# Two attention layers over 32 images: both lanes on one layer at either end, and the setup in parts

## The chip, the cores and the metric

The kernel runs on one core of a Trainium2 chip. The core has a matrix engine (TensorE, PE in the rows), VectorE (DVE), ScalarE (ACT), GpSimd (POOL) and SyncE (SP), which issues DMA transfers; each works through its own queue in order and they meet at semaphores. The metric is the device time of one execution in microseconds (us); lower is better.

## What is computed

x is 32 images of 128 channels by 32x32 pixels, float32. Two layers of self-attention follow one another:

```python
# layer 0
h = group_norm(x, 32 groups) * gn_w + gn_b
q, k, v = split(qkv_w @ h + qkv_b)                  # 128 channels each
attn = softmax(q^T k * C ** -0.5)                   # 1024 x 1024 for each image
x = x + proj_w @ (v attn^T) + proj_b
# layer 1
q, k, v = Wq @ x + bq, Wk @ x + bk, Wv @ x + bv     # 16, 16 and 128 channels
x = gamma * (v softmax(q^T k)^T) + x
```

## The kernel before

**Tiles.** One image has N = 1024 pixels; its attention is done in 8 tiles (TILES) of 128 rows of the 1024x1024 matrix. A tile runs through these steps: scores (TensorE, `score0` or `score1`) into a PSUM tensor `scores[l]` of 1024 columns; row maximum (VectorE, `row_max`, L498); exponent (ScalarE); a split into a float16 head and a float16 tail in `rows[l]`; a DMA transpose into a ring of four, `pt[l]` (SP, `swing`); 24 matmuls with V's head and tail (`attend`, L710 to L712); a division by the row sum (`invert` on VectorE, `norm` on ScalarE); a transpose back on TensorE (`back`, L731); and an addition on VectorE (`x1_out` or `y_out`). To keep float32's accuracy in float16 matmuls, each product of layer 0 is three matmuls (head by head, head by tail, tail by head).

**Lanes.** There are two lanes with buffers of their own. Lane 0 takes layer 0, lane 1 takes layer 1. Lane 0 puts its exponents into `prob` (L397), so that its scores are free right after, and splits on GpSimd (`head_row0` L300, `tail_row0` L305). Lane 1 writes its exponents over the scores (L402) and splits on ScalarE (L409) and VectorE (L512), so its scores are free only when the tail is done. `score0` (two halves of 512 columns, three matmuls each) and `score1` (two matmuls) are the layers' own.

**Slots.** The queue of each engine is written out slot by slot (an image has eight), in Python, with all loops unrolled. The constants of L33 to L42 say at which slot from the image's start a step stands: lane 0's tile t has its exponent in slot 8n+t, lane 1's in slot 8n+t+13 (EXP, L34); both lanes attend three slots after the exponent (L36) and add four after it (L37). Before image n's tiles come its load (-16), the statistics (-12, -11), two products for the group norm (-10, -9), the root (-8, GpSimd), `h` in float32 (GpSimd) and its head (ScalarE, -7), its tail (GpSimd, -6), four projections to q and k (-5, -4, -3, 0), each with a copy on ScalarE and a split on GpSimd, and V (1, 2). Layer 1's q and k are projected at 7 and 11, its V at 12 and 14. All layer-0 projections of q and k, the products of the norm and the transposes back go through one PSUM bank, `bank_t`; the V and layer-1 projections through another, `bank_w`.

**Order in a TensorE slot (L813 to L842).** Attend for both lanes; V or a layer-1 projection; q/k projection; norm product; the first half of lane 0's scores for the next slot, lane 1's scores, the second half of lane 0's; a wait until `bank_t` has been read; the transposes back. ScalarE's slot (L456) is lane 1's exponent and head, lane 0's exponent, the heads and copies out of PSUM, `h_head`, then the norms of both lanes.

**Setup.** Weights are loaded by SP behind image 0 (L258 to L267), turned by TensorE (`setup`, L796), scaled and split by VectorE (`setup`, L581); TensorE, VectorE and ScalarE do the whole of it between the first eight slots and all the others (L662, L844, L488 to L492).

## Time and profile before

| | us |
|---|---|
| median of 3 runs | 1636.66 |
| lowest and highest | 1635.16, 1637.1 |
| the profiled execution | 1633.07 |
| its span | 1630.8 |

The span is the time from the first to the last instruction of the profiled execution; 2.3 us lie around it. Busy time of the engines over the span: TensorE 1519.8, VectorE 1289.7, GpSimd 1247.4, ScalarE 1209.0 us. The page counts 43555 instructions and 305 MB of DMA, of which 512 transposes and 32 images in and out. The clock granted to TensorE was 0.988 of the full one on average. Time is best read by slots: the exponents (L397 for lane 0, L402 for lane 1) mark where each slot stands.

### The profile page before, as it was taken

How to read it: one execution, taken by the hardware profiler on the slowest of the kernel's cores; microseconds unless marked ns; L12 is line 12 of the kernel's file. 1: busy time of each engine (PE TensorE's matmuls, PEld its weight loads, DVE VectorE, ACT ScalarE, POOL GpSimd, SP SyncE). 2: the span in 40 equal slices, each digit the busy share in tenths (PEclk: the TensorE clock that was granted, in tenths of full speed). 3: DMA queues.
4: the chain of work that ended last, by engine and by line, in shares of the span. 5: the costliest groups of instructions: out<-in, count | busy, mean ns of one | idle time of the engine just before them, and what ended most of it. 6: DMA issues, size and time to landing. Idle time of an engine off the chain costs nothing.

```text
span 1630.8 us, 43555 instructions
## 1 busy us (share of the span) xinstructions
PE 1519.8 (93%) x16777; PEld 1102.4 (68%) x16777; DVE 1289.7 (79%) x2499; ACT 1209.0 (74%) x1697; POOL 1247.4 (76%) x1036
## 2 busy tenths in 40 slices
PE   3789999999999999999999999999999999999975
PEld 1557777767777677776767777677677777767754
DVE  2478888888888888888888888888888888887854
ACT  1467887777777777777777777877777877777753
POOL 3998888887888887787888788788878888877600
PEclk9999999999999999999999999999999999999987
DMA  1689999999999999999999999999999999999974
GB/s 47 117 143 200 196 198 201 209 192 201 195 201 204 198 196 196 197 198 192 203 203 204 203 190 204 198 198 205 190 203 194 195 205 197 203 189 186 195 137 97
DMA packets 1081437, 305.19 MB, mean 187 GB/s; under 512 B 1068273, under 2 KB 1068945, under 8 KB 1081233
## 3 DMA queue, kind: packets, MB, share of 16 engines
q1 hardware_dynamic: 1080080, 302.41, 106.1%
q8 instruction: 135, 2.21, 0.5%
q14 instruction: 70, 0.57, 0.1%
q10 hardware_dynamic: 1152, 0.00, 0.0%
HBM read 17.13 MB, written 16.78 MB: 21 GB/s over the span
## 4 chain that ended last, share of the span: by engine, by line
PE 48%; ACT 22%; DVE 16%; issue 10%; POOL 2%; DMA 1%; SPq 1%; ACTq 0%; POOLq 0%; DVEq 0%
DVE nmax L498 10%; ACT scores L402 9%; ACT prob L397 8%; PE mixed L710 7%; PE mixed L712 7%; PE mixed L711 7%; PE scores L671 6%; PE bank_w L778 4%; PE scores L673 4%; PE scores L672 4%; PE scores L696 3%; PE bank_t L731 2%; ACT v_head L452 2%; PE bank_w L768 2%; DVE qk L563 1%
## 5 line engine op out<-in xcount | busy, mean ns | idle before, releaser
L710 PE MATMUL mixed<-v_head,pt 128*128 128x129 f16 x4096 | 722.6, 223 | 4.5 <-DMA pt<-rows 4.3
L712 PE MATMUL mixed<-v_head,pt 128*128 128x129 f16 x4096 | 722.5, 220 | 0.0
L711 PE MATMUL mixed<-v_tail,pt 128*128 128x128 f16 x4096 | 722.2, 219 | 0.0
L498 DVE TENSOR_REDUCE nmax<-scores 128x1 f32<-128x1024 f32 x512 | 602.4, 1216 | 52.6 <-PE scores L696 32.3
L305 POOL TENSOR_TENSOR rows<-prob,rows 128x1024 f16<-128x1024 f32 x256 | 545.5, 2131 | 21.3
L402 ACT ACTIVATE scores<-scores,nmax 128x1024 f32<-128x1024 f32 x256 | 278.6, 1088 | 279.4 <-DVE nmax L498 279.4
L300 POOL TENSOR_SCALAR rows<-prob 128x1024 f16<-128x1024 f32 x256 | 267.9, 1046 | 227.3 <-ACT prob L397 210.8
L512 DVE SCALAR_TENSOR_TENSOR rows<-scores,rows 128x1024 f16<-128x1024 f32 x256 | 313.6, 1225 | 153.3 <-ACT rows L409 153.2
L711 PEld LDWEIGHTS mixed<-v_tail,pt 128*128 128x128 f16 x4096 | 407.0, 99 | 2.7
L710 PEld LDWEIGHTS mixed<-v_head,pt 128*128 128x128 f16 x4096 | 400.2, 98 | 7.0 <-DMA pt<-rows 6.6
L712 PEld LDWEIGHTS mixed<-v_head,pt 128*128 128x128 f16 x4096 | 398.1, 97 | 0.0
L397 ACT ACTIVATE prob<-scores,ebias 128x1024 f32<-128x1024 f32 x256 | 283.9, 1109 | 29.5 <-DVE ebias L503 25.9
L409 ACT ACTIVATE rows<-scores 128x1024 f16<-128x1024 f32 x256 | 262.2, 1024 | 23.7 <-ACT scores L402 0.4
L671 PE MATMUL scores<-qk_head 128*128 128x512 f16 x512 | 197.9, 387 | 48.7 <-ACT prob L397 47.9
L673 PE MATMUL scores<-qk_head,qk_tail 128*128 128x512 f16 x512 | 194.5, 380 | 0.0
L672 PE MATMUL scores<-qk_tail,qk_head 128*128 128x512 f16 x512 | 194.4, 380 | 0.0
L414 ACT ACTIVATE normal<-mixed,rinv 128x128 f32<-128x128 f32 x512 | 161.7, 371 | 22.3 <-DVE rinv L508 22.2
L671 PEld LDWEIGHTS scores<-qk_head 128*128 128x128 f16 x512 | 50.4, 99 | 158.5 <-issue 77.7
L364 POOL TENSOR_TENSOR qk_tail<-qk,qk_head 128x512 f16<-128x512 f32 x128 | 148.3, 1158 | 10.7
L731 PEld LDWEIGHTS bank_t<-ident,normal 128*128 128x128 f32 x512 | 69.7, 140 | 78.7 <-ACT normal L414 17.2
L696 PE MATMUL scores<-qk 64*128 64x512 f16 x512 | 100.5, 389 | 22.3 <-DVE rows L512 21.7
L731 PE MATMUL bank_t<-ident,normal 128*128 128x128 f32 x512 | 109.7, 286 | 6.7 <-ACT normal L414 6.6
(90 smaller groups left out, 1847.0 us busy)
## 6 DMA issues: line engine op xcount, KB each, us to landing
x_raw<-in_x_dram SPq DMA_DIRECT2D x32, 512.0 KB, 4.8
out_dram<-y SPq DMA_DIRECT2D x64, 256.0 KB, 3.0
pt<-rows SPq DMA_TRANSPOSE x512, 4.9
w_qkv<-in_L_conv_qkv_w_dram SPq DMA_DIRECT2D x3, 64.0 KB, 3.8
b_qk<-in_L_conv_bk_dram SPq DMA_DIRECT2D x8, 0.1 KB, 1.9
b_qk<-in_L_conv_bq_dram SPq DMA_DIRECT2D x8, 0.1 KB, 1.6
w_proj<-in_L_conv_proj_w_dram SPq DMA_DIRECT2D x1, 64.0 KB, 3.5
w_v<-in_L_conv_Wv_dram SPq DMA_DIRECT2D x1, 64.0 KB, 3.4
```

Of the source, the lines that this page charges most:

```text
L300: nc.gpsimd.tensor_scalar(rows[0][:, t % 2, 0, :], prob[:, t % 2, :], 1.0, 1.0, ALU.mult, ALU.mult).then_inc(row_headed[0], 1)
L305: nc.gpsimd.tensor_tensor(rows[0][:, t % 2, 1, :], prob[:, t % 2, :], rows[0][:, t % 2, 0, :], ALU.subtract).then_inc(row_tailed[0], 1)
L397: nc.scalar.activation(prob[:, t % 2, :], scores[0][:, :], ACT.Exp, bias=ebias[:, t:t + 1], scale=1.0).then_inc(exped[0], 1)
L402: nc.scalar.activation(scores[1][:, :], scores[1][:, :], ACT.Exp, bias=nmax[1][:, t:t + 1], scale=1.0).then_inc(exped[1], 1)
L409: nc.scalar.activation(rows[1][:, t % 2, 0, :], scores[1][:, :], ACT.Copy, scale=P_UP).then_inc(row_headed[1], 1)
L498: nc.vector.reduce_max(nmax[layer][:, t:t + 1], scores[layer][:, :], AX.X, negate=True).then_inc(maxed[layer], 1)
L512: nc.vector.scalar_tensor_tensor(out=rows[1][:, t % 2, 1, :], in0=scores[1][:, :], scalar=P_UP, in1=rows[1][:, t % 2, 0, :], op0=ALU.mult, ...
L671: mm(dst, a_head, b_head, start=start, stop=False)
L673: return mm(dst, a_tail, b_head, start=False, stop=stop)
L710: mm(mixed[l][:, 0:C + 1], head, vh[:, im.p, m, 0:C + 1], start=(m == 0), stop=False)
L711: mm(mixed[l][:, 0:C], head, vt[:, im.p, m, :], start=False, stop=False)
L712: done = mm(mixed[l][:, 0:C + 1], tail, vh[:, im.p, m, 0:C + 1], start=False, stop=(m == TILES - 1))
```

## The change

Tiles are no longer tied to a lane by layer. A class `Tile` has a layer, an image, a number and a lane; `tiles_of_lane` deals them out. Images 0 and 1 of layer 0 put their even tiles in lane 0 and their odd ones in lane 1 and so take four slots each; images 30 and 31 of layer 1 do the same. All others stay as they were, with layer 1 of image n starting at slot 9+8n. The last tile is in slot 256. Counts of semaphores go by a tile's number in its lane (`tile.i`) or by a step's number in its list (`Steps`). `x_raw` gets a third buffer. The order of the steps in a slot stays; a lane-1 tile of layer 0 has all its six score matmuls between the halves of lane 0's. The setup is cut: the turning of weights and q/k's part of VectorE's work come before slot -8; the rest of VectorE's stands after slot -5, of TensorE's after slot -3. ScalarE no longer waits for the setup before image 0's `h_head`, and loads its activation table with a small activation at the start. The four semaphore pairs of `bank_w` become one (`w_made`, `w_tailed`).

```diff
+X_BUFS = 3
+PAIRED = 2
+SWING, ATTEND, ADD = (1, 0), 3, 4
+FIRST_SLOT, SETUP_SLOT = -16, -8
+HEADED, DVE_SETUP, PE_SETUP, SET_UP = -6, -4, -2, -1
+
+def start0(n):
+    return n * TILES // 2 if n < PAIRED else (n - PAIRED // 2) * TILES
+
+def start1(n):
+    early = start0(PAIRED) + 1 + n * TILES
+    return early if n < IMAGES - PAIRED else start1(IMAGES - PAIRED - 1) + TILES + (n - IMAGES + PAIRED) * TILES // 2
...
+def tiles_of_lane(lane):
+    tiles = []
+    for layer, start, paired in ((0, start0, range(PAIRED)), (1, start1, range(IMAGES - PAIRED, IMAGES))):
+        for n in range(IMAGES):
+            for t in range(TILES):
+                if n in paired and t % 2 == lane:
+                    tiles.append(Tile(layer, n, t, lane, start(n) + t // 2))
+                elif n not in paired and layer == lane:
+                    tiles.append(Tile(layer, n, t, lane, start(n) + t))
...
+LOADS = Steps(-16)
+STATS = Steps(-12, -11)
+GN = Steps(-10, -9)
+ROOT, H_FULL = Steps(-8, first={1: (-7,)}), Steps(-7, first={1: (-6,)})
+H_HEAD, H_TAIL = Steps(-7, first={1: (-6,)}), Steps(-6, first={1: (-5,)})
+X_BIAS = Steps(-5, first={0: (0,), 1: (-1,), 2: (0,), 3: (-4,)})
+QK = Steps(-5, -4, -3, 0, first={0: (-5, -4, -3, -2), 1: (-4, -3, -2, -1)})
+QK_SPLIT = Steps(-4, -3, -2, 1, first={0: (-5, -5, -4, -1), 1: (-3, -2, -1, 0)})
+V_SLOTS = {0: (-1, 0), 1: (-1, 0)}
+QK1_SLOTS = {0: (6, 7), 1: (8, 11), IMAGES - 1: (10, 11)}
+V1_SLOTS = {0: (8, 11), 1: (9, 10), IMAGES - 1: (13, 14)}
+W = Steps(1, 2, 11, 15, 12, 14,
+          first={n: V_SLOTS.get(n, (1, 2)) + QK1_SLOTS.get(n, (11, 15)) + V1_SLOTS.get(n, (12, 14))
+                 for n in (0, 1, IMAGES - 1)})
+X1_BIAS = Steps(15, first={0: (9,), IMAGES - 1: (12,)})
+STORE = Steps(lambda n: start1(n) + 9, lambda n: start1(n) + 13,
+              first={n: (lambda n: start1(n) + 6, lambda n: start1(n) + 8)
+                     for n in range(IMAGES - PAIRED, IMAGES)})
...
             def load_x(im):
-                if im.at_least(2):
-                    sp.wait_ge(x_biased, im.n - 1)
+                if im.at_least(X_BUFS):
+                    sp.wait_ge(x_biased, im.n - X_BUFS + 1)
...
             for dst, src in loads:
-                sp.dma_start(dst, src).then_inc(setup_loaded, 16)
+                sp.dma_start(dst, src).then_inc(w_loaded, 16)
...
# ScalarE
-            body(whole(FIRST_IT))
+            act.wait_ge(consts_made, 8)
+            nc.scalar.activation(warm[:, :], minus_half[:, :], ACT.Exp)
+            every_slot(body, FIRST_SLOT, HEADED)
             act.wait_ge(setup_loaded, 16 * N_LOADS)
+            act.wait_ge(setup_dve, SETUP_DVE_QK)
+            every_slot(body, HEADED, SET_UP)
             act.wait_ge(setup_dve, SETUP_DVE_ALL)
-            act.wait_ge(consts_made, 8)
-            every_iteration(body)
+            every_slot(body, SET_UP)
...
# VectorE
-            body(whole(FIRST_IT))
-            setup()
-            every_iteration(body)
+            every_slot(body, FIRST_SLOT, SETUP_SLOT)
+            setup_qk()
+            every_slot(body, SETUP_SLOT, DVE_SETUP)
+            setup()
+            every_slot(body, DVE_SETUP)
...
# TensorE
             def v_project(im, h):
-                if h == 1:
-                    pe.wait_ge(v_tailed, im.n * 2 + 1)
-                elif im.at_least(1):
-                    pe.wait_ge(qk1_tailed, im.n * 2 - 1)
+                pe.wait_ge(h_tail_done, im.n + 1)
+                pe.wait_ge(h_head_done, im.n + 1)
+                bank_w_read()
...
+                first, second = (lane.get(slot + 1) for lane in TILE_AT)
+                if first and first.layer == 0:
+                    score0(first, 0)
+                elif first:
+                    score1(first)
+                if second and second.layer == 1:
+                    score1(second)
+                elif second:
+                    score0(second, 0)
+                    score0(second, 1)
+                if first and first.layer == 0:
+                    score0(first, 1)
+                evicted_here(slot)
...
-            body(whole(FIRST_IT))
-            setup()
-            every_iteration(body)
+            every_slot(body, FIRST_SLOT, SETUP_SLOT)
+            setup_turns()
+            every_slot(body, SETUP_SLOT, PE_SETUP)
+            setup()
+            every_slot(body, PE_SETUP)
```

## Rows read from the trace of the kernel before

**Rows 1.** The page, busy us (share of the span) and instructions of each engine.

```profile
PE 1519.8 (93%) x16777; PEld 1102.4 (68%) x16777; DVE 1289.7 (79%) x2499; ACT 1209.0 (74%) x1697; POOL 1247.4 (76%) x1036
```

**Rows 2.** The windows by stage: length, busy us (instructions) of each engine, PEclk, DMA, GB/s.

```profile
38.00:98.00 60.00, 48.84 (x422) 31.10 (x423) 28.86 (x60) 29.52 (x42) 56.88 (x46) 0.94 0.58 106
98.00:1550.00 1452.00, 1407.64 (x15821) 1023.45 (x15819) 1211.72 (x2321) 1138.08 (x1602) 1174.13 (x961) 1.00 1.13 198
1550.00:1615.00 65.00, 43.02 (x428) 35.75 (x426) 35.95 (x60) 33.07 (x44) 2.33 (x2) 0.79 0.68 122
```

**Rows 3.** The waits from 400 to 1400 us: total us, times, longest.

```profile
ACT scores L402 <- DVE nmax L498: 178.3, 167, 1.8
...
POOL rows L300 <- DMA pt<-rows: 11.7, 10, 1.8
```

**Rows 4.** The timeline of ScalarE, exponents of four slots: start, length in us.

```profile
37.84 1.11 ACT L397 ACTIVATE prob<-scores,ebias 128x1024 f32<-128x1024 f32 x1 [6.33 <-DVE ebias L503]
...
97.77 1.09 ACT L402 ACTIVATE scores<-scores,nmax 128x1024 f32<-128x1024 f32 x1 [1.49 <-DVE nmax L498]
...
1550.45 1.09 ACT L402 ACTIVATE scores<-scores,nmax 128x1024 f32<-128x1024 f32 x1 [0.50 <-DVE nmax L498]
...
1614.99 1.09 ACT L402 ACTIVATE scores<-scores,nmax 128x1024 f32<-128x1024 f32 x1 [1.36 <-DVE nmax L498]
```

**Rows 5.** The page's loads of x (median to landing), then the timeline of the start.

```profile
x_raw<-in_x_dram SPq DMA_DIRECT2D x32, 512.0 KB, 4.8
...
5.14 1.29 DVE L537 BATCH_NORM_STATS2 stats<-x_raw 128x6 f32<-128x512 f32 x2 [5.14 <-DMA x_raw<-in_x_dram]
...
8.27 0.56 PE L793 MATMUL bank_t<-gs,group_mean 128*128 128x1 f32 x2 [0.79 <-DVE gs L553]
...
11.94 14.01 SPq L229 DMA_DIRECT2D x_raw<-in_x_dram  x2
...
21.04 1.24 ACT L441 ACTIVATE h_head<-x_raw,gs 128x1024 f16<-128x1024 f32 x1
26.21 0.69 ACT L423 ACTIVATE qk<-bank_t,b_k 128x512 f32<-128x512 f32 x1 [3.93 <-PE bank_t L673]
...
24.73 0.58 PE L671 MATMUL bank_t<-h_head,w_head 128*128 128x512 f16 x1 [5.32 <-POOL h_tail L335]
...
25.54 0.63 PE L673 MATMUL bank_t<-h_head,w_tail 128*128 128x512 f16 x1
27.04 0.58 PE L671 MATMUL bank_t<-h_head,w_head 128*128 128x512 f16 x1 [0.87 <-ACT qk L423]
...
39.24 0.38 PE L672 MATMUL scores<-qk_tail,qk_head 128*128 128x512 f16 x1
```

**Rows 6.** The timeline of one light double slot, TensorE, then ScalarE.

```profile
1034.14 0.38 PE L671 MATMUL scores<-qk_head 128*128 128x512 f16 x1 [0.29 <-ACT prob L397]
...
1034.88 0.39 PE L696 MATMUL scores<-qk 64*128 64x512 f16 x2
...
1036.36 0.22 PE L710 MATMUL mixed<-v_head,pt 128*128 128x129 f16 x1
...
1039.93 0.38 PE L671 MATMUL scores<-qk_head 128*128 128x512 f16 x1
...
1036.58 1.09 ACT L402 ACTIVATE scores<-scores,nmax 128x1024 f32<-128x1024 f32 x1 [0.44 <-DVE nmax L498]
...
1038.68 1.11 ACT L397 ACTIVATE prob<-scores,ebias 128x1024 f32<-128x1024 f32 x1
```

**Rows 7.** The page's groups of GpSimd: count, busy us, mean ns.

```profile
L305 POOL TENSOR_TENSOR rows<-prob,rows 128x1024 f16<-128x1024 f32 x256 | 545.5, 2131 | 21.3
...
L300 POOL TENSOR_SCALAR rows<-prob 128x1024 f16<-128x1024 f32 x256 | 267.9, 1046 | 227.3 <-ACT prob L397 210.8
...
L364 POOL TENSOR_TENSOR qk_tail<-qk,qk_head 128x512 f16<-128x512 f32 x128 | 148.3, 1158 | 10.7
```

**Rows 8.** The timeline of TensorE, its last transpose back.

```profile
1627.70 0.30 PE L731 MATMUL bank_t<-ident,normal 128*128 128x128 f32 x1 [0.75 <-ACT normal L414]
```

## What the change does to the time, predicted

> **What bounds the kernel now.** I read the page first. TensorE is busy for 93% of the span, the next engine for 79% [rows 1]. The windows then cut the span into the stages of the schedule [rows 2]. The reader is to see four: a setup before 38 us in which nothing is full; 38 to 98 us, where lane 1 has no tiles yet and GpSimd is busy for 56.88 of 60 us; 98 to 1550 us, with both lanes, where TensorE is busy for 1407.64 of 1452 us; and 1550 to 1615 us, lane 1 alone, where TensorE is busy for 43.02 of 65 us and nothing is full. The waits say what paces the middle: ScalarE waits for VectorE's maximum in every slot, 178.3 us in 167 slots [rows 3], so behind the full TensorE lies a ring that is nearly as long. In the last stage the maximum, the two ScalarE passes, the tail on VectorE and the next scores follow one another with nothing beside them.
>
> Pace of the stages, from the ScalarE rows [rows 4]. Slot 0's exponent starts at 37.84, slot 13's (lane 1) at 97.77, slot 256's at 1550.45, slot 268's, the last, at 1614.99. The 13 lane-0 slots thus cost 59.9 us, 4.6 each; the 243 double ones 5.978 each; the last ones 5.38. From the last exponent to the end of the span are 15.8 us.
>
> **What the change does to the count.** Before, lane 1 runs 13 slots behind lane 0, so 269 slots: 26 with one tile and 243 with two. After, images 0 and 1 put even tiles in lane 0 and odd ones in lane 1 (slots 0 to 7), slot 8 has lane 0 alone, slots 9 to 247 have layer 0 beside layer 1, slot 248 has lane 1 alone, and images 30 and 31 fill both lanes in slots 249 to 256. That is 257 slots, 255 with two tiles. The work is the same. What goes is 24 half-filled slots, what comes is 12 full ones; of the 255, 8 hold layer 0 twice and 8 layer 1 twice. The stage prices decide.
>
> **Setup.** Before, image 0's h_head waits for the whole setup and an activation table load, then runs at 21.04; the first projection starts at 24.73 [rows 5]. After, the table load hangs on a constant and h_head on the group norm alone, some 2.3 behind its second product (8.27), so h_head (1.24) runs at about 10.6 and h_tail (2.13, as the tail of the same shape [rows 7]) ends near 14.1. But the projection doesn't start there: the first slot's queue on TensorE has image 1's statistics product ahead of it. Image 1's load is issued at 11.94, behind the 23 setup loads on SP, and lands about 4.8 us later [rows 5], so 16.7. For image 0, statistics, aggregate, first product and VectorE's three steps took from 5.14 to 8.27, 3.1. The first projection then starts at 19.8, 4.9 earlier than before. The four projections follow at 2.3 (24.73 to 27.04), with a second product of 1.0 after the first. TensorE's rest of the setup is queued behind the third, and waits with VectorE's in turns: a product and two steps of VectorE twice over, of the size of the statistics' product and steps, some 2.4. Projection 4 starts at 30.0 and its copy ends 2.2 later; image 2's statistics product with its steps (1.3), the first half of V (12 matmuls, 1.3 at this clock) and another product 0.6 stand before the scores, which start at 35.3. So the rest of the setup costs TensorE's queue 2.4, and pulling image 2 ahead another 1.9: of 9 us of shorter start, little is left. The scores of tile 0's first half and of tile 1 are 9 matmuls of 512 columns. Before 38.9 these took 0.63 and stood over 0.4 apart (0.81 for two, 24.73 to 25.54), 512 columns at the 1.2 GHz level; at 39.24 they take 0.38, as in the middle at 0.22 apart [rows 5, 6]. So 3.7; then the maximum (1.23). **The first exponent, lane 1's, starts at 40.2**, and lane 0's 2.1 later, against 37.84 before: slot 0 starts late, but with two tiles.
>
> **A slot with layer 0 in both lanes** is not in the trace. Its ring comes from a light double slot [rows 6]: exponent of lane 1 at 1036.58, lane 0's at 1038.68, free score bank at 1039.8, scores from 1039.93, and the next maximum when lane 1's are done. In that order lane 1's scores stand between the halves of lane 0's, so the ring holds 3 matmuls of lane 0 (0.74), 2 of layer 1 and the maximum; it closes in 5.79 (1034.14 to 1039.93). With layer 0 in lane 1 there are 6 matmuls in place of 2, at 0.215 apart: +0.9, so 6.7. GpSimd is not longer: lane 1's split runs on ScalarE and VectorE, and GpSimd has a tile (3.2) and, per slot, up to two of its splits (1.8 each) or h steps (1.2 and 2.1) [rows 7]; that is 26 us in slots 1 to 4, against 29 of the ring. The head of a split and the h steps have no row here; I size them by the head and tail of a tile, half of it for 512 columns. TensorE's own work in such a slot is 0.5 (turning back) + 2.73 (two attends, 1036.36 to 1039.09) + 2.6 (scores), plus 0.65 for each projection or half of V, and some 0.9 for each of layer 1's [rows 6]. Slots 0 to 2 have no attend: ring, 3 x 6.7 = 20.1. Slot 3 holds two projections in one bank; the second waits for the copy of the first, which ScalarE does only after lane 0's exponent and V's head (0.69 for the copy [rows 5], about as much for V's head), and the next scores queue behind it: 6.7 + 2.2 = 8.9. Slot 4 has V and a projection, 7.2; slot 5 6.7; slot 6 has layer 1's first projection and a statistics product, 7.4. Slots 7 and 8 (the latter with one tile): 4.0 to the scores of slot 8, 1.3 scores, 0.5 + 2.73 + 0.95 (half of layer 1's V, an estimate as above) + 0.65 of queue, 2.6 from the scores to the exponent, 12.7 in all. Slot 9's exponent comes at 40.2 + 20.1 + 8.9 + 7.2 + 6.7 + 7.4 + 12.7 = **103.2**.
> Bounds of the eight slots: no better than the light double slot, 5.8 each; no worse than the same ring with its nine matmuls at the 1.2 GHz spacing, 8.65 each. I take 6.7 to 8.9, slot by slot, since the rows of full clock are the nearest: slot 1's scores before, at 39.24, were already at 0.38.
>
> **The middle** doesn't change: every step keeps its place in the cycle of eight slots. Lane 1 starts its image in phase 1 and not 5; layer 1's two projections swap phases (11 and 15 for 7 and 11: 3 and 7 either way), stores swap likewise. Added are waits on semaphores that have long been reached (V on h, on the W bank), and the bank waits in one count. The third x_raw buffer takes away a wait that costs nothing: no row has anything waiting for x in the middle. I cost all of it at 0, within 0.02 per slot (5 us, the range takes it). 240 slots (9 to 248) at 5.978 = 1434.7, less 0.6 for slot 248, which has one tile: **slot 249 at 1537.3**.
>
> **A slot with layer 1 in both lanes:** the light slot's ring with 2 matmuls where lane 0 had 3, 5.79 - 0.22, and 5.5 taken; it can't be under 5.38 (lane 1 alone) or, with TensorE at about 4.1 us of work, over 5.98. Seven of them to slot 256, with 0.5 for layer 1's projections in 250 and 251: 39.0, **1576.3**. Image 31's projections are in place one slot before they are needed, and image 29's last store lands about 0.6 before y's half is written again, by the SP order; if it is late, under 2 us.
>
> **The drain** was 15.8 with one attend in each of the last slots, each followed by a pause for ScalarE's norm and the turning back, 0.75 + 0.30 [rows 8]. Now there are two, 1.36 more each; the first is partly under the last exponents. Lane 0's last tile ends its exponent 2.1 later and its split on GpSimd takes 3.2 where lane 1's needs 1.02 + 1.23. From the last lane-1 exponent: attends of three slots, each 2.73 + 1.15 of latency, from 4.7 on, then 3.1 for add and store: 19.4. Span 1576.3 + 19.4 = 1595.7.
>
> **The sum against before's span**: slot 9 at 103.2 for 97.77 of the old slot 13 (+5.4), 3 double slots fewer (-17.9), -0.6 for the single one, seven slots of 5.5 with their extras in place of 12 of 5.38 (-25.5), drain +3.6: -35.0. The profiled execution has 1630.8 of span in 1633.07, and the median of the three runs, 1636.66, is 3.6 over that. 1595.7 + 2.3 + 3.6 = 1601.6; I say 1602.
>
> **A rule against the change.** The granted clock fell to 0.94 in 38 to 98 us and to 0.79 in the last stage, where TensorE had been busy for two thirds of the time, and stood at 1.00 in the middle [rows 2]. The Trainium skill, "TensorE: Matmul & The Clock Gate", section "Part 1: The HAM clock gate", says that the throttled state is the default and that only sustained activity releases it. By that, the start, where each burst of scores follows a pause, could stay at half clock. By that rule the trace agrees for the first 38 us. Without the page the same case stands on rows 2 and 5, as the first rival.
>
> **The rivals.**
> 1. Half clock at the start. Slots 0 to 7 keep the 1.2 GHz spacing because TensorE has pauses of over 2 us in slots 0 to 2. Price: up to 8.65 - 6.7 = 1.95 a slot, 15.6 over the forecast if it lasts for all eight, 8 for half: 1610 to 1617. For: this was so until 38.9, and 0.94 later. Against: before, slot 1 was at full clock right after such a pause. Chance 0.17. That the two lanes don't overlap at all (two tiles at the lone lane-0 slot's 4.6, 9.2 a slot) would give 1602 + 20, 1622; 0.02 of the chance is for that.
> 2. The start goes at the pace of the middle: the ring is not the bound since ScalarE's order gives slack, slot 3's stall is hidden: eight slots at 5.8 to 6.0, 8 to 13 us less: 1589 to 1594. For: 5.79 is what a light double slot takes. Against: 0.9 of matmuls more in the ring. Chance 0.14.
> 3. Slower. The place is GpSimd's head of lane 0, which waits for the transposes two tiles back to leave its rows: 11.7 us in 10 times in the middle window, 1.8 at most [rows 3]. If the shift of lane 1's image against lane 0's makes one such wait of 1.8 in every image in place of 0.56, 30 images cost 37 us and the time is 1639. It decides from 1.16 more an image. Against: stores, loads and transposes keep their order in the cycle. Chance 0.04.
> The forecast, within 1594 to 1610, has 0.65.
>
> **The numbers.** The range is 1588 to 1615: below lies what is left of rival 2, above the worst of rival 1 and rival 3. A measurement here can tell about 0.2% (3.3 us) from no change. Faster 0.95 (the forecast, rivals 1 and 2), same 0.01, slower 0.04.
>
> **What would show it.** Lane 1's first exponent at 40, the first projection at 19.8 behind image 1's statistics, a gap of 2 us in TensorE's scores after slot 3, exponents 6.7 to 7.4 apart in slots 0 to 6, slot 9 at 103, 47.8 us per image after it, 5.5 apart in slots 249 to 256 and a drain of 19. The prediction is wrong if an image in the middle costs over 48.3 or under 47.4, or if the slots of the start leave 5.8 to 8.65.

## The result and the profile after

| | before, us | after, us |
|---|---|---|
| median | 1636.22 | 1597.99 |
| lowest and highest (4 runs each) | 1635.16, 1637.1 | 1595.75, 1598.88 |
| the profiled execution | 1633.07 | 1598.83 |
| its span | 1630.8 | 1597.1 |

The ratio of after to before on record is 0.9765, with a 95% interval of 0.9748 to 0.9782: 38 us less, where 34.7 had been forecast (1602 for 1636.66). In the profiled executions alone the spans differ by 33.7. The profiled execution before lies 2.1 us under the lowest timed run of its kernel and the one after at the top of its own, so the account below, made on spans, ends 4.5 us short of the medians' difference.

The page of the kernel after, busy us and instructions of each engine, against [rows 1]:

```profile
PE 1507.5 (94%) x16777; PEld 1095.0 (69%) x16777; DVE 1289.0 (81%) x2499; ACT 1205.5 (75%) x1698; POOL 1245.6 (78%) x1036
```

The same 16777 matmuls and 2499 VectorE instructions; one instruction more on ScalarE, the small activation that brings the table in. Nothing of the work went, so the gain is time in which engines stood half empty. TensorE's busy time is 12.3 us shorter for the same matmuls because fewer of them ran at a lowered clock (0.988 of the full one granted before, 0.997 after). The clock is a small part of the 33.7 us all the same. The 12 lone lane-1 steps of before lie between 5.3 and 5.5, inside and outside of stretches with a granted clock of 0.50, so it costs at most 0.2 a step there. The 13 lone lane-0 slots took 59.9 us, and the kernel with only its end paired (below) takes 56.5 for them once its own low-clock steps are set right, so at most 3.5. Against that, the kernel after has 2.8 us of such steps itself.

The windows of the kernel after, by stage: length, busy us (instructions) of each engine, granted clock, DMA share, GB/s; the first three against [rows 2], the fourth is the drain:

```profile
38.00:98.00 60.00, 49.49 (x461) 32.27 (x459) 39.68 (x68) 38.24 (x50) 43.91 (x39) 0.97 0.80 143
102.00:1536.00 1434.00, 1391.70 (x15667) 1013.47 (x15665) 1196.37 (x2293) 1122.88 (x1584) 1152.02 (x943) 1.00 1.13 197
1536.00:1577.00 41.00, 32.23 (x395) 25.98 (x393) 33.42 (x60) 29.54 (x41) 22.20 (x15) 0.96 1.03 187
1577.00:1597.00 20.00, 13.30 (x182) 12.33 (x179) 5.62 (x21) 5.56 (x11) 4.29 (x3) 0.91 0.76 152
```

In 38 to 98 us GpSimd is down from 56.88 to 43.91 us, and VectorE and ScalarE up from 28.86 and 29.52 to 39.68 and 38.24: lane 1's splits run on those two. The middle has the ratio of before (TensorE busy for 97%). The last stage takes 41 us where it took 65, at a clock of 0.96 for 0.79.

The exponents of lane 1 in the kernel after (the timeline of ScalarE; start and length in us, and in brackets the idle time before it), slots 0 to 4, 9 and 249, and the last three, against [rows 4]:

```profile
39.77 1.09 ACT L447 ACTIVATE scores<-scores,nmax 128x1024 f32<-128x1024 f32 x1 [4.79 <-DVE nmax L546]
46.39 1.09 ACT L447 ACTIVATE scores<-scores,nmax 128x1024 f32<-128x1024 f32 x1 [2.41 <-DVE nmax L546]
54.31 1.09 ACT L447 ACTIVATE scores<-scores,nmax 128x1024 f32<-128x1024 f32 x1 [3.07 <-DVE nmax L546]
60.99 1.09 ACT L447 ACTIVATE scores<-scores,nmax 128x1024 f32<-128x1024 f32 x1 [2.89 <-DVE nmax L546]
69.57 1.09 ACT L447 ACTIVATE scores<-scores,nmax 128x1024 f32<-128x1024 f32 x1 [2.00 <-DVE nmax L546]
...
101.74 1.09 ACT L447 ACTIVATE scores<-scores,nmax 128x1024 f32<-128x1024 f32 x1 [1.03 <-DVE nmax L546]
...
1536.59 1.09 ACT L447 ACTIVATE scores<-scores,nmax 128x1024 f32<-128x1024 f32 x1 [1.02 <-DVE nmax L546]
...
1558.71 1.09 ACT L447 ACTIVATE scores<-scores,nmax 128x1024 f32<-128x1024 f32 x1 [1.02 <-DVE nmax L546]
1565.78 1.09 ACT L447 ACTIVATE scores<-scores,nmax 128x1024 f32<-128x1024 f32 x1 [1.37 <-DVE nmax L546]
...
1576.62 1.09 ACT L447 ACTIVATE scores<-scores,nmax 128x1024 f32<-128x1024 f32 x1 [1.06 <-DVE nmax L546]
```

The eight starts between 39.77 and 89.78 are 6.62, 7.92, 6.68, 8.58, 6.85, 6.68 and 6.68 apart, and slot 9 follows 11.96 behind slot 7. From slot 9 to slot 249 are 1434.85 us in 240 slots. The last eight starts are 5.26, 5.82, 5.83, 5.21, 7.07, 5.59 and 5.25 apart. Two steps stand out that no row of the work explains, 46.39 to 54.31 and 1558.71 to 1565.78. The windows of the kernel after show them (columns as above):

```profile
46.40:49.50 3.10, 0.00 (x0) 0.00 (x0) 2.17 (x3) 3.07 (x4) 2.88 (x3) 0.90 0.91 171
49.50:52.00 2.50, 2.41 (x6) 0.89 (x7) 0.29 (x1) 1.74 (x3) 2.19 (x2) 0.50 1.06 110
1557.70:1561.00 3.30, 3.30 (x30) 3.19 (x30) 2.80 (x6) 2.20 (x3) 2.46 (x2) 0.50 0.97 194
```

TensorE does nothing in 46.4 to 49.5, since the next scores wait for lane 0's exponent, and the six score matmuls behind the pause run at a granted clock of 0.50, the 1.2 GHz level. The same level is granted in 1557.7 to 1561.0, in a stage in which TensorE is busy for 32.23 of 41 us. I call such a stretch a half-clock stretch below. A third one falls into the drain (1581.5 to 1584.9).

The account on spans, against [rows 4]: slot 9 stands at 101.74 where slot 13 stood at 97.77, +4.0. 240 double slots for 243: 1434.85 for 1452.68, -17.8. 40.03 us in the last stage for 64.54: -24.5. A drain of 20.5 for 15.8: +4.7. Sum -33.6, and the spans differ by 33.7 (roundings).

### The profile page after: what moved, and what is told of

Its sections match the earlier page's. It is cut to its first block and busy times, and to the rows that moved or that the text cites. A ratio compares the mean times of both kernels' runs of the same rounds, so it can differ in the third digit from the quotient of the medians.

```text
span 1597.1 us, 43928 instructions
## 1 busy us (share of the span) xinstructions
PE 1507.5 (94%) x16777; PEld 1095.0 (69%) x16777; DVE 1289.0 (81%) x2499; ACT 1205.5 (75%) x1698; POOL 1245.6 (78%) x1036
## 5 line engine op out<-in xcount | busy, mean ns | idle before, releaser
L769 PE MATMUL mixed<-v_head,pt 128*128 128x129 f16 x4096 | 714.9, 222 | 0.0
L771 PE MATMUL mixed<-v_head,pt 128*128 128x129 f16 x4096 | 714.7, 219 | 0.0
L770 PE MATMUL mixed<-v_tail,pt 128*128 128x128 f16 x4096 | 714.6, 218 | 0.0
L412 POOL TENSOR_TENSOR qk_tail<-qk,qk_head 128x512 f16<-128x512 f32 x128 | 148.0, 1157 | 10.6
```

The source lines that it names most:

```text
L769: mm(mixed[l][:, 0:C + 1], head, vh[:, p, m, 0:C + 1], start=(m == 0), stop=False)
L770: mm(mixed[l][:, 0:C], head, vt[:, p, m, :], start=False, stop=False)
L771: done = mm(mixed[l][:, 0:C + 1], tail, vh[:, p, m, 0:C + 1], start=False, stop=(m == TILES - 1))
```

## The experiments

Each ratio is to runs of the kernel before on the same chip, between and beside the others. Each edit is made to the kernel after.

### Only the start paired

All of layer 1 goes back to one lane; images 30 and 31 take 16 slots.

```diff
-    return early if n < IMAGES - PAIRED else start1(IMAGES - PAIRED - 1) + TILES + (n - IMAGES + PAIRED) * TILES // 2
+    return early
...
-    for layer, start, paired in (..., (1, start1, range(IMAGES - PAIRED, IMAGES))):
+    for layer, start, paired in (..., (1, start1, ())):
```

> Only the start is paired (images 0 and 1 of layer 0 in both lanes, the setup in parts); images 30 and 31 of layer 1 stay in lane 1, whose last tile moves to slot 264. Theory (the gain is the idle halves of slots that pairing fills, and pairing the start alone only moves them: lane 0 is done four slots earlier and lane 1 is alone for 17 slots in place of 13): slot 9 at 101.7 as in the changed kernel, 239 double slots at 5.98 to slot 248 at 1531, 16 lone steps of 5.38 to 1617, drain 15.8: span 1632.5 for 1630.8 before, no gain. Rival (each end's pairing brings about half of the gain by itself): span about 1614.

Measured: 1637.53 us (10 runs), ratio 1.0016 (1.0006 to 1.0025), span 1634.1. The start has all that it has in the full change, and slot 9 comes at 99.89 and not at 101.74 mainly because this profile has no half-clock stretch there (its step from slot 1 to 2 is 6.62 for 7.92). Then lane 1 is alone from slot 249 on: the timeline of ScalarE in this kernel, slot 248 and the last exponent, and the window of that stage.

```profile
1529.56 1.09 ACT L445 ACTIVATE scores<-scores,nmax 128x1024 f32<-128x1024 f32 x1 [0.50 <-DVE nmax L544]
...
1616.16 1.09 ACT L445 ACTIVATE scores<-scores,nmax 128x1024 f32<-128x1024 f32 x1 [1.58 <-DVE nmax L544]
```

```profile
1531.00:1617.00 86.00, 54.02 (x502) 43.65 (x500) 46.58 (x74) 43.70 (x57) 1.12 (x1) 0.75 0.66 118
```

The sum against before: slot 9 +2.1, 239 double slots for 243 -23.0 (1429.67 for 1452.68), 16 lone slots of 5.41 for 12 of 5.38 +22.1 (86.6 for 64.54), drain +2.1, together +3.3. So packing the first two images alone brings nothing: lane 1 has 256 tiles of layer 1 to get through whatever comes before, and what is saved ahead is idle time of lane 0 behind.

### Only the end paired

Lane 0 starts alone with the new setup, 13 slots ahead; images 30 and 31 of layer 1 are dealt to both lanes.

```diff
 def start0(n):
-    return n * TILES // 2 if n < PAIRED else (n - PAIRED // 2) * TILES
+    return n * TILES
...
 def start1(n):
-    early = start0(PAIRED) + 1 + n * TILES
-    return early if n < IMAGES - PAIRED else start1(IMAGES - PAIRED - 1) + TILES + (n - IMAGES + PAIRED) * TILES // 2
+    early = 13 + n * TILES
+    return early if n < IMAGES - PAIRED else 257 + (n - IMAGES + PAIRED) * TILES // 2
...
-W = Steps(1, 2, 11, 15, 12, 14,
+W = Steps(1, 2, 7, 11, 12, 14,
```

The special steps of image 1, and of the images after it, go as well.

> Only the end is paired (images 30 and 31 of layer 1), lane 0 starts alone as before with the setup in parts; lane 1 runs 13 slots behind and pairs in slots 257 to 264. Theory: first exponent at 33 (nothing of image 1 stands before the first projection, no second tile), 13 lone slots of 4.6 to 93, 240 double ones to 1528, about 16 for the three lone and one empty slot, 40 for the pairs, 20.5 of drain: span 1604, most of the gain. Rival (each end half): 1614. Second rival (the pairs of the end cost more than in the changed kernel because lane 0 comes to them without a break): 1608 or more.

Measured: 1607.08 us, ratio 0.9826 (0.9811 to 0.9841), span 1605.5. Timelines of this kernel: TensorE's first projection; ScalarE's first exponent, slot 13 and the last exponent.

```profile
14.15 0.61 PE L724 MATMUL bank_t<-h_head,w_head 128*128 128x512 f16 x1 [2.29 <-POOL h_tail L383]
```

```profile
32.56 1.11 ACT L442 ACTIVATE prob<-scores,ebias 128x1024 f32<-128x1024 f32 x1 [3.42 <-DVE ebias L552]
...
92.54 1.09 ACT L447 ACTIVATE scores<-scores,nmax 128x1024 f32<-128x1024 f32 x1 [1.49 <-DVE nmax L546]
...
1586.68 1.09 ACT L447 ACTIVATE scores<-scores,nmax 128x1024 f32<-128x1024 f32 x1 [1.06 <-DVE nmax L546]
```

Against before, the last stage (slots 257 to 264) gives 24.0 us (40.52 for 64.54), the new setup 5.2 (slot 13 at 92.54 for 97.77); from slot 13 on, 240 double slots with three lone ones and an empty one take 0.9 more than the 243 double ones (1453.62 for 1452.68), and the drain takes 3.0 back. Without image 1 in its way the first projection runs at 14.15, the time at which the prediction had h_tail ready (14.1), and not at 18.89. Going from here to the full change moves the start: +9.2 at slot 9 against slot 13, -18.8 for the three lone slots and the empty one between the last double slot and the pairs (1434.85 for 1453.62), -0.5 in the last stage and +1.7 in the drain, -8.4. The medians say 9.1. So the two ends are not alike. The end alone, with the new setup, brings -28.1 us in the medians, most of the gain; the start alone costs 2.3; both together bring -38.2. The prices of a pair say why: a pair of layer 1 takes hardly longer than a lone tile (5.2 to 5.8 for 5.38), a pair of layer 0 takes 6.6 to 8.6 where a lone tile takes 4.6. The pairs at the start pay only once the end is paired too. In this profile the first three steps of lane 0 are 5.09, 5.39 and 5.39 where the next is 4.12, with a clock of 0.50 granted from 34.1 to 47.7, so a lone start at full clock would be 3.5 us shorter still.

### The setup in one piece

```diff
-            setup_qk()
-            every_slot(body, SETUP_SLOT, DVE_SETUP)
-            setup()
-            every_slot(body, DVE_SETUP)
+            setup_qk()
+            setup()
+            every_slot(body, SETUP_SLOT)
```

The same on TensorE, and ScalarE waits for all of it ahead of its first slot.

> The changed kernel with the setup in one piece before slot -8 on VectorE and TensorE, and ScalarE waiting for all of it with its table load behind, as before the change; the pairs stay. Theory (the parts hide 2.4 us of TensorE's setup turns no better than before and gain only what lies between 18.9, where image 1's statistics let the first projection go, and 24.7, where the whole setup does, less those 2.4): first projection at 24.7, lane 1's first exponent at 43.2, span 3.4 longer, 1600.5. Rival A (the setup is the gate, 10 us of h_head's move count): span 8 to 10 longer. Rival B (other work covers it): within 0.5.

Measured: 1597.58 us, ratio 0.9771 (0.9757 to 0.9786), span 1596.2. Timelines of this kernel, ScalarE and TensorE:

```profile
17.39 1.28 ACT L488 ACT_TABLE_LOAD   x1 [17.39 <-DVE gam_bv L679]
18.69 1.24 ACT L488 ACTIVATE h_head<-x_raw,gs 128x1024 f16<-128x1024 f32 x1
```

```profile
22.23 0.58 PE L719 MATMUL bank_t<-h_head,w_head 128*128 128x512 f16 x1 [2.65 <-POOL h_tail L383]
```

The first projection is 3.3 later, but the fourth stands at 29.90 for 29.02 and the first exponent at 41.02 for 39.77: 1.25. The parts of the setup are the same work on the same queue; done behind the third projection it costs there about what it costs ahead of the first. Expected was a span 3.4 longer; it is 0.9 shorter, since this profile is 2.0 shorter from slot 249 to its end (58.5 us for 60.5). Even the 1.25 doesn't show in the medians (ratios 0.9771 and 0.9765, intervals overlapping): no difference in time is shown for cutting the setup. In this trace the last stage has no step of 7.07 (the half-clock stretch fell elsewhere), which gives the 1.4 of slot 9 (103.11) back. With only the end paired, where nothing of image 1 stands in the way, the new setup as a whole brings the first exponent from 37.84 to 32.56, but no run there has the setup in one piece.

### Image 1's load first

SP issues it ahead of 16 small loads of biases.

```diff
                 for im, _ in LOADS.at(slot):
-                    load_x(im)
+                    if im.n != 1:
+                        load_x(im)
...
                 sp.dma_start(dst, src).then_inc(w_loaded, 16)
+            load_x(Image(1))
```

> The changed kernel with image 1's load issued right behind the seven weight loads, ahead of the 16 small bias loads. Theory (the first projection waits for image 1's statistics product, which stands ahead of it in TensorE's queue, and that for image 1's load): image 1 lands near 9.5, the first projection is then gated by image 0's h_tail and starts at 14.2 in place of 18.9, the first exponent at 35.1 in place of 39.8, span 4.7 shorter, 1592.4. Rival (the small loads or the setup gate it): less than 1 us.

Measured: 1596.61 us, ratio 0.9755 (0.9738 to 0.9771), span 1595.2. The first exponent came 2.2 earlier (37.61), not 4.7. The timeline of VectorE in this kernel:

```profile
13.51 0.15 DVE L646 TENSOR_SCALAR b_q<-b_q 128x1 f32<-128x1 f32 x1 [2.64 <-DMA b_qk<-in_L_conv_bk_dram]
13.58 1.28 DVE L592 BATCH_NORM_STATS2 stats<-x_raw 128x6 f32<-128x512 f32 x2
```

Image 1 has landed, but its statistics stand in VectorE's queue behind the scaling of b_q, which waits 2.64 us for the small loads that are now later. In the kernel after, x comes last and hides that wait.

### Image 1's load first, and the small loads awaited later

The edit before, and b_q's scaling goes from the first part of VectorE's setup to the second; ScalarE waits for it before slot -3.

```diff
-                dve.wait_ge(setup_loaded, 16 * N_LOADS)
-                nc.vector.tensor_scalar(b_q[:, :], ...).then_inc(setup_dve, 1)
 
             def setup():
+                dve.wait_ge(setup_loaded, 16 * N_LOADS)
+                nc.vector.tensor_scalar(b_q[:, :], ...).then_inc(setup_dve, 1)
```

> As x1_early, and VectorE's wait for the small bias loads (with the scaling of q's bias) moves behind image 1's statistics, to the start of the rest of the setup. Theory (in x1_early the statistics stood behind that wait, which ended at 13.5; with it gone only image 0's h_tail gates the first projection): first projection at 14.2, first exponent at 35.1, 4.7 earlier than in the changed kernel, span 1592.4. Rival (the setup's turns on TensorE and VectorE or ScalarE's wait for the same loads gate it): no more than x1_early's 2.2.

Measured: 1593.42 us, ratio 0.9746 (0.973 to 0.9762), span 1588.8. Timelines of this kernel, TensorE (statistics product, first projection) and ScalarE:

```profile
12.81 0.56 PE L855 MATMUL bank_t<-mv,group_mean 128*128 128x1 f32 x2 [0.71 <-DVE mv L597]
...
14.45 0.58 PE L727 MATMUL bank_t<-h_head,w_head 128*128 128x512 f16 x1 [1.07 <-POOL h_tail L385]
```

```profile
34.71 1.09 ACT L449 ACTIVATE scores<-scores,nmax 128x1024 f32<-128x1024 f32 x1 [4.15 <-DVE nmax L549]
```

The first projection waits for h_tail alone now, as in the kernel with only its end paired, and the first exponent comes 5.06 earlier. The span is 8.3 shorter, more than the edit can account for: this profile, the shortest of the four runs (1590.49 to 1596.12), has no half-clock stretch in slot 1 (1.3) and takes 58.3 from slot 249 to its end (2.2 less). The medians say 4.6, on different chips and with intervals of the ratio that touch those of the kernel after; the gain is shown at the first exponent, not in the time. The rows show the prediction's step "image 1's statistics product stands ahead of the first projection" as the one that held the start back by 4.4 us.

### Image 2's projections in slots of their own

```diff
-QK = Steps(-5, -4, -3, 0, first={0: (-5, -4, -3, -2), 1: (-4, -3, -2, -1)})
+QK = Steps(-5, -4, -3, 0, first={0: (-5, -4, -3, -2), 1: (-4, -3, -2, -1), 2: (-4, -3, -2, 0)})
```

Its splits go with them, one slot behind each.

> Image 2's first three projections stand in slots 4, 5, 6 in place of 3, 4, 5, so that slot 3 has one projection into bank_t and not two. Theory (the second projection of slot 3 waits for ScalarE's copy of the first, and the next scores queue behind it): the step from slot 3 to 4, 8.58 in the changed kernel, becomes 6.7; slot 6 has one projection more and may give back up to 0.65: slot 9 at 99.9 to 100.5 in place of 101.74, span 1.3 to 1.9 shorter. Rival (slot 3 is long for the first attends and their transposes): no change of that step.

Measured: 1598.9 us, ratio 0.978 (0.9766 to 0.9795), span 1599.5. In the kernel after, slot 3's second projection waits for a copy (timeline of TensorE; its first projection stands at 63.58):

```profile
65.52 0.38 PE L724 MATMUL bank_t<-h_head,w_head 128*128 128x512 f16 x1 [1.13 <-ACT qk L470]
```

Without it, the step from slot 3 to slot 4 falls from 8.58 to 7.24. But slot 6, to which a projection was moved, goes from 6.68 to 8.30 (83.59 to 91.89). The timeline of TensorE in the experiment:

```profile
86.64 0.38 PE L724 MATMUL bank_t<-h_head,w_head 128*128 128x512 f16 x1
...
88.25 0.38 PE L852 MATMUL bank_t<-mv,group_mean 128*128 128x1 f32 x2 [0.80 <-ACT qk L470]
```

The cause of the 8.58 is shown (two users of one bank in a slot, with ScalarE's copy between them), and with it that a projection ahead of a norm product is such a pair too. The expected 1.3 to 1.9 us less did not come: the stall changed its slot. Slot 9 even stands 2.1 later (103.86), of which 1.7 is no matter of the order: half-clock stretches at 48.6 to 55.5 and 58.9 to 62.3 make the steps from slot 1 and slot 2 8.52 and 7.76, for 7.92 and 6.68. Nor did the step from slot 3 come down to the 6.7 expected, and what holds the last 0.5 is not shown.

### Lane 1's scores first

Where both lanes hold layer 0, all of lane 1's scores come ahead of lane 0's.

```diff
+                second_first = first and second and first.layer == 0 and second.layer == 0
+                if second_first:
+                    score0(second, 0)
+                    score0(second, 1)
                 if first and first.layer == 0:
                     score0(first, 0)
...
-                elif second:
+                elif second and not second_first:
```

> In slots 0 to 7 all six score matmuls of lane 1 go before lane 0's six, in place of between their halves. Theory (a slot with layer 0 in both lanes is paced by lane 1's ring of exponent, head, tail, six matmuls and maximum, and lane 0's three matmuls stand in it only through the order): 6.25 a slot in place of 6.62 where TensorE has pauses (slots 0 to 2), little where it is full: 1 to 2.5 shorter in all. Rival (TensorE's or GpSimd's own work paces these slots, and lane 0 gets later): no change or longer.

Measured: 1596.35 us, ratio 0.9764 (0.9747 to 0.978), span 1594.5. The first exponent comes at 38.73, 1.04 earlier; the steps are 6.42, 6.57, 6.67, 8.42, 6.86, 6.28, 7.07, and slot 9 stands at 99.16 for 101.74. The seven steps sum to 48.3. This profile has a half-clock stretch too (49.6 to 53.0), so the order is better read where the clock stays up, from two kernels that follow below: `kept_busy` without the order and `best_start_fill` with it. There the steps from slots 0, 1, 2 and 5 are 6.62, 6.62, 6.68 and 6.68 without it and 6.22, 6.22, 6.28 and 6.28 with it, that from slot 6 is 6.68 and 7.06, and the seven sum to 48.7 and 47.4.

So the order brings 0.4 in a slot without a stall and not the 0.65 that three matmuls take. The rows say why: TensorE without the order, then with it (timelines of `kept_busy` and `best_start_fill`), and the tail of lane 1, which frees its scores, with it.

```profile
56.04 0.39 PE L724 MATMUL scores<-qk_head 128*128 128x512 f16 x1 [1.54 <-ACT prob L442]
```

```profile
49.59 0.39 PE L727 MATMUL scores<-qk_head 128*128 128x512 f16 x1 [1.15 <-DVE rows L566]
...
48.31 1.23 DVE L566 SCALAR_TENSOR_TENSOR rows<-scores,rows 128x1024 f16<-128x1024 f32 x1 [0.79 <-ACT rows L457]
```

Without the order lane 0's three matmuls start at 56.04, as soon as its exponent is done, while lane 1's tail runs until 56.24: 0.2 of their 0.65 stood beside the ring all along. With the order TensorE starts right behind lane 1's tail.

### TensorE kept busy

Matmuls that nobody reads, from data at hand, in slots 0 to 2 (8 each), 249 to 255 (3 each) and 256 (8); the output is the same.

```diff
+                if 0 <= slot < 3:
+                    filler(mixed[0], 8)
+                if 249 <= slot < 256:
+                    filler(bank_t, 3)
...
+                if slot == 256:
+                    pe.wait_ge(w_tailed, made["w"])
+                    filler(bank_w, 8)
```

> Matmuls of 512 columns whose result nobody reads fill part of TensorE's pauses: 8 before the scores in slots 0 to 2, 3 in each of slots 249 to 255, 8 in slot 256. Theory (the pauses bring the half-clock stretches, which lengthen the step from slot 1 to 2 to 7.92, one step of the last stage to 7.07, and the drain): no stretch at half clock from slot 1 on, that step 6.65, the last stage's steps 5.9 at most, the drain 19: 1.3 + 1.3 + 1.0 shorter, 3.6 in all. Rival (the half-clock stretches come whatever TensorE does): the steps stay, and the filler costs up to its own length where TensorE has no pause.

Measured: 1596.84 us, ratio 0.977 (0.9755 to 0.9784), span 1595.3. The windows of this kernel for the pause and the scores behind it:

```profile
46.20:49.50 3.30, 1.82 (x9) 0.70 (x8) 2.37 (x3) 3.27 (x4) 2.85 (x4) 1.00 0.92 173
49.50:52.00 2.50, 2.50 (x13) 1.12 (x12) 0.54 (x2) 1.51 (x2) 2.42 (x2) 1.00 0.68 130
```

With 1.82 us of matmuls in the pause the clock is granted in full, and the step from slot 1 to slot 2 is 6.61 for 7.92; that from slot 253 to 254 (1557.06 to 1562.64) is 5.58 for 7.07. So both odd steps are the clock: 1.3 and 1.5 us. The kernels without filler agree: of the seven with both lanes on layer 0 at the start, five have a half-clock stretch that begins between 46.9 and 50.3, and four of these a step of 7.92 to 8.52 with it (in the one with lane 1's scores first it is lane 0's step that is long, 7.28); two have no stretch there and a step of 6.62; none of the four kernels with filler in slots 0 to 2 has one. But the drain grew by 1.0 to 21.5. Of the 2.8 us at slot 256 (1573.78 for 1576.62) 1.8 is left in the span, and of the medians 1.2, which can't be told from nothing (the intervals overlap). Where it went is in the chain that ended last. In the kernel after, that chain runs through the attends of the drain; in this kernel it runs, from 1558.75 on, through SP's issues of transposes (L292; start and length in us; SPq is SP's queue):

```profile
1567.52 3.21 SPq L292
1570.91 3.38 SPq L292
1575.10 2.79 SPq L292
1578.07 1.32 SPq L292
1579.57 3.48 SPq L292
1583.23 4.99 DMA pt<-rows
```

With two lanes there are two transposes a slot, up to 3.5 us each to issue, and that queue is nearly as long as the ring of 5.5. SP's last issue of a transpose ends at 1586.35 here and at 1587.09 in the kernel after (1576.12 and 10.97 for its last four): exponents that come 2.8 earlier make it 0.7 earlier.

But a last stage at full pace alone doesn't bring this about. Two kernels without filler have one as well (38.5 us from slot 249 to 256): the setup in one piece, and image 1's load first with the small loads later. The window of the first from its last half-clock stretch to its end:

```profile
1555.60:1596.20 40.60, 29.45 (x412) 25.51 (x410) 23.21 (x54) 20.60 (x33) 16.98 (x11) 1.00 0.96 186
```

Their chains run through SP's transposes too, but SP's last issue ends 10.75 and 10.47 us behind the last exponent of lane 1 (10.47 in the kernel after), and the time from slot 249 to the end is 58.5 and 58.3 us for 60.5. In the three kernels with filler in slots 249 to 255 it ends 12.4 to 12.6 behind, and slot 249 to the end takes 60.3 to 60.6. So where no half-clock stretch is in the way the end is 2 us shorter, and it is with the filler that SP's queue takes them back. Why SP's issues then take longer isn't shown; nor is it whether SP or the DMA engines behind it set their pace: the DMA share is 0.96 in the window above and 1.03 in the last stage of the kernel after.

### The edits together

`best` has image 1's load first, the small loads awaited later, lane 1's scores first, and the filler in slots 0 to 2 and 249 to 255. `best_no_order` is that without the order of the scores; `best_start_fill` is `best` with filler in slots 0 to 2 alone.

> x1_early_bq and kept_busy's filler in slots 0 to 2 and 249 to 255 (not in slot 256) together. Theory (the edits act on different stretches, so they add): first exponent at 34.7, slot 9 at 95.4, middle 1434.9, no half-clock stretch before the drain, last exponent 1530.3 + 38.7, drain 20: span 1589. x1_early_bq's profile had 1588.8 with its half-clock stretches where they cost least; against its median of 1593.4 the gain is 1 to 3. Rival (the filler costs what it saves): the same median as x1_early_bq.

> The same with lane 1's scores first in slots 0 to 7. Theory (of the order's gain, 1.0 is at the first exponent, whose scores are done three matmuls earlier, and the rest is lost since VectorE's tail of lane 1 stands behind lane 0's maximum, which now comes later): 1 to 1.5 shorter than best_no_order, span 1588. Rival (the order brings 0.37 a slot once the clock stays up): 2.5 to 3 shorter.

> best without the filler in slots 249 to 255; that in slots 0 to 2 stays. Theory (at the end the filler costs what it saves: the last exponent step was 5.82 and 5.9 with it and 5.25 without, the drain 21.5 against 19.8 to 20.5, while one half-clock stretch there costs 0 to 1.5 by where it falls): 0.5 to 1.5 shorter than best's median, 1590.5, last step 5.25, one or two half-clock stretches from 1545 on, and a wider spread of the times. Rival (the filler at the end is worth its stretch): 1 to 1.5 longer, 1593.

| kernel | median, us | ratio to before | interval | first exponent | slot 9 | last exponent, lane 1 | drain |
|---|---|---|---|---|---|---|---|
| after | 1597.99 | 0.9765 | 0.9748 to 0.9782 | 39.77 | 101.74 | 1576.62 | 20.5 |
| best_no_order | 1593.29 | 0.9736 | 0.9723 to 0.9749 | 35.16 | 95.83 | 1570.12 | 21.5 |
| best | 1591.52 | 0.9727 | 0.9714 to 0.974 | 33.91 | 93.85 | 1568.20 | 21.5 |
| best_start_fill | 1591.58 | 0.9746 | 0.973 to 0.9761 | 33.63 | 93.16 | 1566.95 | 21.5 |

`best_no_order` was expected at a span of 1589 and has 1591.6; 1.5 of the 2.6 is the drain, expected at 20. The order of the scores is worth 1.8 us beside the others in the medians (1593.29 to 1591.52, same chip, but the intervals overlap) and 1.9 at the last exponent, between the 1 to 1.5 expected and the rival's 2.5 to 3. The filler at the end brings nothing that shows: the last step, from slot 255 to 256, is 5.26 without it and 5.89 with it (1562.31 to 1568.20), and the medians of `best` and `best_start_fill`, on two chips, are equal within 0.1 us. The drain is 21.5 either way, but not from the same cause: without the filler SP's last issue ends 10.6 behind the last exponent, as in the kernel after, and its transpose takes 6.06 to land, where those of the ten other kernels with their end paired take 4.3 to 5.1; why is not shown. Their ratios differ by one run of 1597.22 in the second and by the kernel before, whose median was 0.9 lower on that chip. The spread is narrower with the filler, 1590.17 to 1593.28 in 4 runs against 1590.23 to 1597.22 in 5, too few to say more. Both are about 6.4 us under the kernel after in the medians; by the intervals of the ratios `best` is shown to be faster than it, `best_start_fill` is not.

## Why the prediction was right

**The count of slots and the middle.** Forecast: 257 slots, 240 of them at 5.978 less 0.6, 1434.1. Measured 1434.85, 47.83 an image, within the 47.4 to 48.3 set as bounds. This holds in every experiment: from slot 9 to slot 249 are 1434.5 to 1435.2 us in all those with both ends paired. The waits in 102 to 1536 us of the kernel after (total us, times, longest) show ScalarE still waiting for the maximum in each slot, against [rows 3]:

```profile
ACT scores L447 <- DVE nmax L546: 258.9, 240, 1.8
```

**The setup.** The first projection was forecast at 19.8 behind image 1's statistics, and came at 18.89: the queue was read rightly, the landing of x1 was put at 4.8 from its issue by the page's median [rows 5] and was 3.7 (12.01 to 15.7). The four projections came at 18.89, 22.12, 24.39 and 29.02 (30.0 for the last), the first exponent at 39.77 (40.2). "Of 9 us of shorter start, little is left" held: at the first exponent the parts are worth 1.25 us. Moving image 1's load and the wait for the small loads, which the change left where they were, gave back 5.06.

**The first eight slots.** Forecast 6.7 each with 8.9 in slot 3, 7.2 in slot 4 and 7.4 in slot 6, then 12.7 for slots 7 and 8. Measured 6.62, 7.92, 6.68, 8.58, 6.85, 6.68, 6.68 and 11.96. The ring of 5.79 + 0.9, taken from the light double slot [rows 6], is within 0.1 of what was measured. Slot 3's stall has the cause that was forecast. Mis-sized were the extras of slots 4 and 6 (7.2 and 7.4, 0.35 and 0.7 too much: the projection and the product fit beside the ring) and slots 7 and 8 (0.7 too much). The half-clock step of 7.92 stands against them, 1.3, and so slot 9 came at 101.74, 1.5 before its forecast, of which 0.4 is from the setup.

**The last stage.** Forecast 39.0, measured 40.03: the ring of 5.5 was right (5.21 to 5.83; without the step of 7.07, which is 1.5 too long by the clock, the sum is 38.5). Slot 256's exponent came at 1576.62 for 1576.3. That it is so near is in part luck: slot 9 came 1.5 sooner than forecast, and the middle took 0.75 and this stage 1.0 longer.

**The drain** was forecast at 19.4 and measured 20.5. With only the end paired it was 18.8 for the same tiles, so the attends were priced 0.6 too high, and the rest is the clock. The timelines of VectorE, additions for the output (L583), in the kernel after and then in that experiment:

```profile
1581.29 0.49 DVE L583 TENSOR_TENSOR y<-bank_t,x1b 128x128 f32<-128x128 f32 x2 [1.07 <-PE bank_t L789]
1586.64 0.49 DVE L583 TENSOR_TENSOR y<-bank_t,x1b 128x128 f32<-128x128 f32 x2 [0.89 <-PE bank_t L789]
1590.35 0.49 DVE L583 TENSOR_TENSOR y<-bank_t,x1b 128x128 f32<-128x128 f32 x2 [0.88 <-PE bank_t L789]
```

```profile
1591.35 0.49 DVE L583 TENSOR_TENSOR y<-bank_t,x1b 128x128 f32<-128x128 f32 x2 [1.07 <-PE bank_t L789]
1595.08 0.49 DVE L583 TENSOR_TENSOR y<-bank_t,x1b 128x128 f32<-128x128 f32 x2 [0.89 <-PE bank_t L789]
```

Two attends with what follows them take 3.73 (forecast 2.73 + 1.15), and 5.35 where they fall into 1581.5 to 1585.0, with a granted clock of 0.52: 1.6, which is 18.8 to 20.4. Not forecast at all was SP's queue of transposes. In the kernel after, its last transpose lands at 1589.14 and the last two attends start at 1590.42, so it had 1.3 us to spare. In the two kernels whose last stage is at full pace without filler (the setup in one piece; image 1's load first, small loads later) that queue is on the chain that ended last, and the drain is 20.0 and 19.8, not 18.8. The last stage and the drain together, 58.4 in the forecast, are 58.5 and 58.3 in those two kernels and 60.5 in the kernel after: without what the clock costs the two terms fit, the second by a path that was not foreseen.

**The range and the offset.** The span came out at 1597.1 for 1595.7, and what I put around it, 2.3 and 3.6 to the median, was too much: 1.7 lie around the span, and the median of the four runs is 0.8 under the profiled one. An offset of one execution to the median of its kernel doesn't carry over to another kernel; without the 3.6 the forecast would have been 1598.0.

**The rivals.** Rival 1, half clock for four to eight slots, didn't happen: it was one step, 1.3 of the 8 to 16 us, and no kernel with filler in the pause has it. The worst of the profiles with both lanes at the start has two such steps (8.52 and 7.76), but the kernel with only its end paired had 0.50 from 34.1 to 47.7, over three lone slots: a long stretch at the start does occur. The Trainium skill, "TensorE: Matmul & The Clock Gate", section "Part 1: The HAM clock gate", says that TensorE's clock goes back to the throttled state after an idle window. The trace agrees for one pause (46.4 to 49.6, then 0.50); the pauses of 2.4 us in slot 0 (40.6 to 43.0) and of 3.3 in slot 2 (54.3 to 57.6) brought no such stretch, so a pause alone doesn't tell. Rival 2, the pace of the middle, is excluded by 6.6 to 6.7 in the slots without a stall, clock at 1.00. Rival 3 turned into its opposite: the waits of the kernel after in 400 to 1400 us have, for the 11.7 us in 10 times of [rows 3],

```profile
POOL rows L348 <- DMA pt<-rows: 0.3, 1, 0.3
```

The shift of lane 1's image by half a cycle took this wait away, and since GpSimd isn't what the slots wait for, it brought nothing.

## What to carry to other kernels

Where two chains of equal length run one behind the other, price a packed slot against a lone one at each end before packing. Here the start alone only moved the idle half to the end (1.0016), since a pair of layer 0 costs half as much again as a lone tile; the end alone, where a pair costs hardly more than a lone tile, brought most of the gain (0.9826, with the new setup); both brought it all (0.9765). A start-up is bounded by what stands ahead of the first useful matmul in the in-order queues: look for the next item's load, product and small-constant waits there (5 us here) before cutting the setup into parts (no difference shown). Before quickening a last stage, see which queue is next in the chain that ended last, here SP's transposes, which took back what a full clock gave once filler matmuls were what gave it.

## What the runs showed of the hardware

- A pause of TensorE of 3.2 us (46.4 to 49.6) was followed by matmuls at the 1.2 GHz level (0.61 to 0.63 us each for 512 columns, 0.38 before), and pauses as long in other slots and runs were not: with the start alone paired, all of slots 0 to 2 are 6.6 to 6.7 apart, without filler. Shorter pauses stood before others: 1.9 us (1554.9 to 1556.8) before the stretch from 1557.6 on, 2.0 (1578.7 to 1580.7) before that from 1581.5 on. Where the stretches fall differs from run to run, and one costs 1.3 to 1.6 us if it falls on the ring or on the attends of the drain. That is about half of the spread of the kernel after (1595.75 to 1598.88); that it makes the spread is not shown.
- The granted clock in the profile reads 1.00 over the first 38 us of the kernels before and after, and yet matmuls of 512 columns take 0.63 us there and stand 0.43 apart (34.85, 35.28 and 35.71 in the kernel after), the 1.2 GHz level; from 38.7 on they take 0.38 and stand 0.21 apart. At the start the durations, not the clock's column, tell the level.
- Issuing a transpose took SP's queue between 1.32 and 3.48 us (the chain of the kernel kept busy), and its queue was nearly full there: with the pauses between them five took 13.12 us from 1553.37 on in that kernel, 2.6 each, 5.2 a slot against a ring of 5.5.
- 16 loads of a few bytes each held SP's queue for 7.4 us, 0.46 each, and a load of x of 512 KB 0.43. The timeline of SP in the kernel with image 1's load first, that load, the small loads, the load of image 2:

```profile
4.55 0.43 SPq L279 DMA_DIRECT2D x_raw<-in_x_dram  x1
5.02 1.82 SPq L317 DMA_DIRECT2D b_qk<-in_L_conv_bk_dram  x4
6.88 3.66 SPq L317 DMA_DIRECT2D b_qk<-in_L_conv_bq_dram  x8
10.59 1.81 SPq L317 DMA_DIRECT2D b_qk<-in_L_conv_bk_dram  x4
12.44 0.42 SPq L279 DMA_DIRECT2D x_raw<-in_x_dram  x1
```
